# Attention on one Trainium2 core: where TensorE transposes k, before or behind q's projection

## The chip, the core and the metric

The kernel is written in Bass for one core of a Trainium2 chip. The engines named here are PE (TensorE, matmuls and transposes), ACT (ScalarE), DVE (VectorE), POOL (GpSimd) and SP (SyncE, which issues most DMAs). Each runs its own instructions in the order written; semaphores tie them together. The metric is the device time of one execution in microseconds. The kernel before takes 3183.95 us (median of three runs, 3183.66 to 3187.36).

## The reference

A vector of conditions is turned into a gate for x, and the gated x goes through two layers of local attention and a gated feed-forward network; the input is added at the end. All in float32. Cut to the layer:

```python
x: (2, 2048, 512)          # B, N, DIM; 8 heads of 64, windows of 256
x2 = cond(x)               # q.k of the condition, clipped to 0..1, gates v; then Wo
for l in range(2):
    h = shift_token(x2)
    q, k, v = split(h @ wqkv[l])               # 512 columns each
    q, k = l2norm(q) * q_scale, l2norm(k) * k_scale
    q, k = rotary_xpos(q, k)
    o = local_attention(q, k, v)               # softmax over two windows of 256, masked
    x2 = x2 + o @ wo[l]
    h = layernorm(shift_token(x2)) * ln_g + ln_b
    a, g = split(h @ w1[l] + b1[l])
    x2 = x2 + (a * gelu(g)) @ w2[l] + b2[l]
return x + x2
```

## The kernel before, in words

The 4096 rows (2 batches of 2048) are cut into 32 tiles of 128. Stages follow each other: the condition, then for each layer the attention over all 32 tiles, then the feed-forward network in 8 blocks of 4 tiles. Float32 products are made of three passes on rounded parts (`three_passes`, L343 to L347): each operand is split into hi, which ACT copies out of PSUM, and lo, which DVE makes as the difference. So a transpose on PE has two followers: ACT's `a_KT_hi`, `a_QT_hi`, `a_hT_hi` (L1035, L1030, L1026), then DVE's `a_KT_lo`, `a_QT_lo`, `a_hT_lo` (L1332, L1327, L1322).

The attention is a software pipeline written out by hand: `body()` on each engine runs through `STEPS` (t from -1 to 32), and one iteration does pieces of several tiles. On PE an iteration is, in this order: the rest of tile t-1's product with V (`pv`), half of tile t's scores, `p_T(t, 0)`, `v_project(t + 1)`, `p_T(t, 1)`, then the part that is changed, then `pv(t, 0)`, `scores(t + 1, 0)`, `p_T(t, 2)`, `k_project(t + 2)`, `p_T(t, 3)` and `project_out(t - 1)`. The changed part is `k_T(t + 1)` (four transposes of the normed k, L580), `q_project(t + 2)` (12 matmuls, L345 to L347), `q_T(t + 1)` and `h_T(t + 3)` (four transposes each, L580). Below, "the iteration of tile x" is the one with t + 1 = x, in which k and q of tile x are transposed and half of its scores are made.

What the parts wait for: `k_T` for `a_k_normed` (DVE L1317, whose factors POOL's `norms` makes); `pv`'s second half for `a_KT_lo`; `scores` for `a_KT_hi`, `a_KT_lo`, `a_QT_hi` and `a_QT_lo` of its tile. ACT's `body()` has its own fixed order in the same place: `k_T`, `square(0, t + 2)` (the square of the projected q, L1013), `q_T`, `h_T`, `q_copy` (L1017). DVE's is `k_T`, `q_T`, `h_T`. Neither is touched by the change.

At a layer's start, in the iteration of tile 0, there is no softmax work yet: PE does `v_project(0)`, `k_T(0)`, `q_project(1)`, `q_T(0)`, `h_T(2)` and `scores(0, 0)`; the last also waits for POOL's `clear_carry` (four memsets, L1673 and L1674). `q_project(1)` writes bank 2, which the stage before used as well.

Of the kernel before, what the change touches and what calls it, by code (L numbers as in the profile page):

```python
# [25 lines left out]
QUAD = 4  # L26
# [3 lines left out]
START = 1  # L30
# [29 lines left out]
def adaln_ffn_program(nc, x, cond, wqT, bq, wk, bk, wvT, bv, woT, bo,  # L60
# [12 lines left out]
    TILES = B * TB  # L73
    BLOCKS = TILES // QUAD
# [28 lines left out]
    def sem(name):  # L103
        sems.append(ctx.enter_context(nc.semaphore(name)))
        return sems[-1]
# [7 lines left out]
    with ctx:  # L113
# [157 lines left out]
        f_out_set = sem("f_out_set"); f_stored = [sem(f"f_stored{i}") for i in range(QUAD)]  # L271
# [30 lines left out]
        def here(x):  # L302

            return 0 <= x < TILES
# [271 lines left out]
        def _(pe):  # L576
            def transpose_tile(dst, src):

                for k in range(KT_):
                    mm = pe.transpose(dst[:, k * P:(k + 1) * P], src[:, k * P:(k + 1) * P], ident[:])  # L580
                return mm
# [92 lines left out]
            def attention(l):  # L674
                G = l * TILES

                def h_T(x):
                    pe.wait_ge(a_h_in[x % QUAD], START + (l * BLOCKS + x // QUAD + 1) * 32)
                    if x == 1:
                        pe.wait_ge(a_hT_lo, START + G + 1)  # L680
                    if x == 2:
                        pe.wait_ge(a_hT_lo, START + G + 2)
                    if x >= 3:
                        pe.wait_ge(a_PT_lo, START + (G + x - 3) * PAIRS + 2)
                    transpose_tile(h_turn, a_h[:, x % QUAD, :]).then_inc(a_hT_mm, 1)

                def q_T(x):
                    pe.wait_ge(a_q_rotated, START + G + x + 1)
                    if x == 0:
                        pe.wait_ge(a_hT_lo, START + G + 2)  # L690
                    else:
                        pe.wait_ge(a_PT_lo, START + (G + x - 1) * PAIRS + 2)
                    transpose_tile(q_turn, a_qrot[:]).then_inc(a_QT_mm, 1)

                def k_T(x):
                    pe.wait_ge(a_k_normed, START + G + x + 1)
                    if x >= 2:
                        pe.wait_ge(a_O_sum[1], START + GROUPS * (G + x - 1))
                    transpose_tile(k_turn, a_krot[:]).then_inc(a_KT_mm, 1)

                def project(which, x, dst, done):
                    if x == 0:
                        pe.wait_ge(a_w_lo, START + 4 * l + W_ORDER.index(which) + 1)
                    for k in range(KT_):
                        mm = three_passes(pe, dst[:], [a_hT[i][:, x % 2, k, :] for i in range(2)],
                                          [a_w[which][i][:, k, :] for i in range(2)], k == 0, k == KT_ - 1)
                    mm.then_inc(done, 1)
# [10 lines left out]
                def q_project(x):  # L718
                    if x == 0:
                        pe.wait_ge(a_k_copied, START + G + 1)  # L720
                        pe.wait_ge(a_k_squared, START + G + 1)
                    else:
                        pe.wait_ge(a_hT_hi, START + G + x + 1)
                        pe.wait_ge(a_hT_lo, START + G + x + 1)
                    if x >= 2:
                        pe.wait_ge(a_S_masked, START + (G + x - 2) * H + H // 2 + 1)
                    project(0, x, q_work(x), a_q_mm)
# [25 lines left out]
                def scores(x, g):  # L753
                    j = x % QUAD
                    if g == 0:
                        if x == 0:
                            pe.wait_ge(a_carry_zero, START + 4 * l + 4)
                            if l == 0:
                                pe.wait_ge(c_o_set, START + TILES)
                            else:  # L760
                                pe.wait_ge(f_out_set, START + l * BLOCKS * QUAD)
                        elif j == 0:
                            pe.wait_ge(a_carried, START + (l * (BLOCKS - 1) + x // QUAD) * 64)
                        for ready in (a_QT_hi, a_QT_lo, a_KT_hi, a_KT_lo):
                            pe.wait_ge(ready, START + G + x + 1)
                    pe.wait_ge(a_S_masked, START + (G + x) * H + g * H // 2)
                    for i in (2 * g, 2 * g + 1):
                        if i == 3 and x >= 2:
                            pe.wait_ge(a_out_set, START + G + x - 1)
                        if i == 1 and here(x + 1):  # L770
                            pe.wait_ge(a_q_copied, START + G + x + 2)
                            pe.wait_ge(a_q_squared, START + G + x + 2)
                        for step, (q_part, k_part) in enumerate(((0, 0), (0, 1), (1, 0))):
                            for odd in range(2):
                                r = slice(odd * HD, odd * HD + HD)
                                mm = pe.matmul(score_bank(2 * i + odd)[:, 0:WIN * P], a_QT[q_part][r, x % 2, i, :],  # L776
                                               a_KT[k_part][r, i, j * P:(j + WIN) * P], start=(step == 0), stop=(step == 2))
                                if step == 2:
                                    mm.then_inc(a_S_mm, 1)
# [17 lines left out]
                def pv(x, g):  # L797
                    if g == 0:
                        pe.wait_ge(a_V_hi, START + G + x + 1)
                        pe.wait_ge(a_V_lo, START + G + x + 1)  # L800
                        if here(x + 1):
                            pe.wait_ge(a_V_lo, START + G + x + 2)
                    elif here(x + 2):
                        pe.wait_ge(a_k_copied, START + G + x + 3)
                        pe.wait_ge(a_k_squared, START + G + x + 3)
                    pe.wait_ge(a_PT_hi, START + (G + x) * PAIRS + 2 * g + 2)
                    pe.wait_ge(a_PT_lo, START + (G + x) * PAIRS + 2 * g + 2)
                    for odd in range(2):
                        pe.wait_ge(a_O_sum[odd], START + GROUPS * (G + x) + g)
                        if odd == 1 and g == 0 and here(x + 1):  # L810
                            pe.wait_ge(a_KT_lo, START + G + x + 2)
                        for i in range(2):
                            for kb in range(WIN):
                                mm = pe.matmul(o_banks[odd][:, i * 2 * P:(i + 1) * 2 * P],  # L814
                                               a_V[:, x % QUAD + kb, 4 * g + 2 * i + odd, :, :].rearrange("p c d -> p (c d)"),
                                               a_PT[:, 2 * i + odd, kb, :, :].rearrange("p c n -> p (c n)"),
                                               start=(kb == 0), stop=(kb == WIN - 1))
                        mm.then_inc(a_PV_mm[odd], 1)
# [11 lines left out]
                def body():  # L830
                    for t in STEPS:
                        if here(t - 1):
                            pv(t - 1, 1)
                        if here(t):
                            scores(t, 1)
                            p_T(t, 0)
                        if here(t + 1):
                            v_project(t + 1)
                        if here(t):
                            p_T(t, 1)  # L840
                        if here(t + 1):
                            k_T(t + 1)
                        if here(t + 2):
                            q_project(t + 2)
                        if here(t + 1):
                            q_T(t + 1)
                        if here(t + 3):
                            h_T(t + 3)

                        if here(t):  # L850
                            pv(t, 0)
                        if here(t + 1):
                            scores(t + 1, 0)
                        if here(t):
                            p_T(t, 2)
                        if here(t + 2):
                            k_project(t + 2)
                        if here(t):
                            p_T(t, 3)
                        if here(t - 1):  # L860
                            project_out(t - 1)
# [892 lines left out]
```

## Time and profile before

| what | value |
|---|---|
| median of three runs | 3183.95 us |
| the profiled execution, its own time | 3186.28 us |
| its span, first to last instruction | 3184.1 us |
| PE busy | 3071.0 us, 96% of the span |
| DVE, ACT, POOL busy | 58%, 47%, 32% |
| mean granted clock of PE | 0.982 of full speed |

The span is what the profile covers; 2.2 us of the execution lie around it. Busy time says how long an engine had an instruction under way. Matmuls overlap on PE (one starts before the last has ended), so steps between the starts of matmuls say what one costs, not its length. A timeline row gives start, length from first start to last end, engine, line, operation, tiles and count of merged instructions, and in brackets how long the engine had been idle and who ended that.

### The profile page before, as it was taken

To read this page: it belongs to the slowest core of one execution; us is meant where nothing else is said; L and a number is where in the kernel's file an instruction comes from. 1 tells how busy PE (TensorE), PEld (TensorE's weight loads), DVE (VectorE), ACT (ScalarE), POOL (GpSimd) and SP (SyncE) were. 2 spreads that over 40 slices of the span, in tenths; PEclk is the share of its full clock that TensorE was granted. 3 is DMA by queue.
4 is the path that set the end of the run, shared out by engine and by line. 5 is a ranking of instruction groups with operands and counts; after the bars stand their busy time and mean duration, and the time that the engine had idled before them with its cause. 6 is when DMAs were issued, how large, how long until landed. Compare 5 with 4: busy or idle time off the path is not lost.

```text
span 3184.1 us, 48197 instructions
## 1 busy us (share of the span) xinstructions
PE 3071.0 (96%) x16534; PEld 2561.8 (80%) x16534; DVE 1838.7 (58%) x3933; ACT 1484.5 (47%) x3198; POOL 1032.2 (32%) x1671
## 2 busy tenths in 40 slices
PE   9998999999968999999999999999986999999999
PEld 8986888888857788888877888888875788887887
DVE  4655888888864333333324888888875344333432
ACT  2116888888852111111113888888882111111111
POOL 1306666666635000000044566666647000000000
PEclk8999999999989999999999999999997999999999
DMA  4421111222123111100131122111114110111110
GB/s 152 140 78 36 65 60 67 67 67 67 54 77 93 40 40 40 40 8 33 40 121 41 57 68 67 59 65 67 61 59 131 53 36 25 53 47 53 54 40 20
DMA packets 149778, 194.49 MB, mean 61 GB/s; under 512 B 23286, under 2 KB 90998, under 8 KB 149284
## 3 DMA queue, kind: packets, MB, share of 16 engines
q1 hardware_dynamic: 133700, 175.69, 16.8%
q10 hardware_dynamic: 15840, 15.73, 1.5%
q8 instruction: 137, 2.24, 0.3%
q14 instruction: 101, 0.83, 0.1%
HBM read 120.06 MB, written 41.95 MB: 51 GB/s over the span
## 4 chain that ended last, share of the span: by engine, by line
PE 95%; DVE 2%; issue 1%; POOL 1%; ACT 1%; DVEq 0%; SPq 0%; ACTq 0%; POOLq 0%
PE bank L345 25%; PE bank L347 25%; PE bank L346 24%; PE bank L814 6%; PE bank L793 6%; PE bank L776 5%; PE bank L580 3%; PE bank L869 1%; DVE a_PT L1363 0%; PE bank L588 0%; DVE f_h L1481 0%; PE bank L605 0%; ACT a_PT L1074 0%; DVE f_hraw L1489 0%; ACT f_hT_hi L1155 0%
## 5 line engine op out<-in xcount | busy, mean ns | idle before, releaser
L1174 ACT ACTIVATE f_gate<-bank,f_b 128x512 f32<-128x512 f32 (+1 forms) x176 | 121.4, 690 | 997.2 <-PE bank L347 997.1
L345 PE MATMUL bank<-f_hT_hi,f_w_hi 128*128 128x512 f32 (+1 forms) x1408 | 556.5, 395 | 16.3 <-ACT f_hT_hi L1155 15.0
L1517 DVE SCALAR_TENSOR_TENSOR f_uraw<-bank,f_b,f_gate 128x512 f32<-128x512 f32 (+1 forms) x176 | 132.1, 751 | 750.7 <-ACT f_gate L1174 750.5
L347 PE MATMUL bank<-f_hT_hi,f_w_lo 128*128 128x512 f32 (+1 forms) x1408 | 552.9, 393 | 0.0
L346 PE MATMUL bank<-f_hT_lo,f_w_hi 128*128 128x512 f32 (+1 forms) x1408 | 552.0, 392 | 0.0
L345 PEld LDWEIGHTS bank<-f_hT_hi,f_w_hi 128*128 128x128 f32 (+1 forms) x1408 | 260.9, 185 | 78.4 <-ACT f_hT_hi L1155 15.7
L347 PEld LDWEIGHTS bank<-f_hT_hi,f_w_lo 128*128 128x128 f32 (+1 forms) x1408 | 260.6, 185 | 64.2
L346 PEld LDWEIGHTS bank<-f_hT_lo,f_w_hi 128*128 128x128 f32 (+1 forms) x1408 | 261.0, 185 | 62.5
L1069 ACT ACTIVATE a_P<-a_S,a_bias 128x384 f32<-128x384 f32 x512 | 309.4, 611 | 3.9 <-DVE a_bias L1352 3.8
L1352 DVE CUSTOM_DVE_ANT_0 a_S<-bank,a_masks,a_q 128x384 f32<-128x384 f32 x512 | 295.7, 615 | 24.0 <-PE bank L776 18.9
L1062 ACT ACTIVATE a_P<-a_P,a_inv 128x384 f32<-128x384 f32 x512 | 287.3, 613 | 2.1 <-DVE a_inv L1358 0.5
L345 PE MATMUL bank<-f_w_hi,f_u_hi 128*128 128x512 f32 (+1 forms) x704 | 277.6, 394 | 5.1 <-issue 4.3
L1363 DVE TENSOR_TENSOR a_PT<-bank,a_PT 128x768 fp32r<-128x768 f32 x256 | 245.2, 958 | 61.6 <-ACT a_PT L1074 59.0
L347 PE MATMUL bank<-f_w_hi,f_u_lo 128*128 128x512 f32 (+1 forms) x704 | 276.2, 392 | 0.0
L346 PE MATMUL bank<-f_w_lo,f_u_hi 128*128 128x512 f32 (+1 forms) x704 | 275.5, 391 | 0.0
L1074 ACT ACTIVATE a_PT<-bank 128x768 fp32r<-128x768 f32 x256 | 207.8, 812 | 83.0 <-PE bank L793 82.8
L793 PE MATMUL bank<-ident,a_P 128*128 128x128 f32 x1536 | 218.5, 279 | 16.3 <-DVE a_PT L1363 12.1
L793 PEld LDWEIGHTS bank<-ident,a_P 128*128 128x128 f32 x1536 | 174.6, 141 | 66.0 <-ACT a_P L1062 35.4
L1651 POOL CAST a_wk_hi<-a_stage 128x512 fp32r<-128x512 f32 x8 | 5.0, 672 | 686.5 <-DMA a_stage<-in_L_ffn_wqkv 686.5
L814 PE MATMUL bank<-a_PT,a_V 128*128 128x256 f32 x1536 | 212.2, 288 | 9.5 <-DVE a_PT L1363 9.3
L814 PEld LDWEIGHTS bank<-a_PT,a_V 128*128 128x128 f32 x1536 | 198.6, 193 | 16.0 <-issue 10.8
L1521 DVE TENSOR_TENSOR f_u_lo<-f_uraw,f_u_hi 128x512 fp32r<-128x512 f32 (+1 forms) x176 | 127.3, 724 | 122.9 <-ACT f_u_hi L1178 122.9
(166 smaller groups left out, 6559.9 us busy)
## 6 DMA issues: line engine op xcount, KB each, us to landing
a_h<-x_layer_in SPq DMA_DIRECT2D x128, 128.0 KB, 2.8
a_res<-x_layer_in SPq DMA_DIRECT2D x64, 256.0 KB, 2.9
x_after_attention<-out_tiles SPq DMA_DIRECT2D x64, 256.0 KB, 2.0
f_res<-x_after_attention SPq DMA_DIRECT2D x64, 256.0 KB, 3.4
f_stage<-in_L_ffn_w SPq DMA_DIRECT2D x60, 256.0 KB, 3.6
a_V<-a_V SPq DMA_DIRECT2D x28, 512.0 KB, 5.1
f_h<-x_after_attention ACTq DMA_DIRECT2D x28, 512.0 KB, 4.5
c_x<-in_x SPq DMA_DIRECT2D x32, 256.0 KB, 3.1
```

The costliest lines, as they stand in the source:

```text
L345: pe.matmul(dst, w[0], m[0], start=start, stop=False)
L346: pe.matmul(dst, w[0], m[1], start=False, stop=False)
L347: return pe.matmul(dst, w[1], m[0], start=False, stop=stop)
L776: mm = pe.matmul(score_bank(2 * i + odd)[:, 0:WIN * P], a_QT[q_part][r, x % 2, i, :], a_KT[k_part][r, i, j * P:(j + WIN) * P], start=(step ...
L793: mm = pe.transpose(pt_banks[:, odd, kb * P:(kb + 1) * P], a_P[:, (2 * i + odd) % 4, kb * P:(kb + 1) * P], ident[:])
L814: mm = pe.matmul(o_banks[odd][:, i * 2 * P:(i + 1) * 2 * P], a_V[:, x % QUAD + kb, 4 * g + 2 * i + odd, :, :].rearrange("p c d -> p (c d)" ...
L1062: act.activation(a_P[:, h % 4, :], a_P[:, h % 4, :], ACT.Copy, scale=a_inv[:, x % 2, h:h + 1])\
L1069: act.activation(a_P[:, h % 4, :], a_S[h % 2][:], ACT.Exp, bias=a_bias[:, h % 2:h % 2 + 1], scale=-1.0, accum_out=a_sum[:, x % 2, h:h + 1] ...
L1074: act.activation(a_PT[:, 2 * (i % 2):2 * (i % 2) + 2, :, 0, :], pt_banks[:, :, 0:WIN * P].rearrange("p h (k n) -> p h k n", k=WIN), ACT.Co ...
L1352: dve.tensor_tensor_reduce(a_S[b][:], score_bank(h)[:, 0:WIN * P], a_masks[:, min(x % TB, 2), :], a_q8[:, x % 2, h:h + 1], 3.0e38, ALU.add ...
L1363: dve.tensor_tensor(a_PT[:, r, :, 1, :], pt_banks[:, :, 0:WIN * P].rearrange("p h (k n) -> p h k n", k=WIN), a_PT[:, r, :, 0, :], ALU.subt ...
L1517: dve.scalar_tensor_tensor(f_uraw[0:ROWS[m], m % 2, :], bank[pair_of(u, m, end)][0:ROWS[m], :], f_b1[0:ROWS[m], 0, m:m + 1], f_gate[0:ROWS ...
```

## The change

`k_T(t + 1)` moves from before `q_project(t + 2)` to behind it. PE then has the transposes of k, q and h in one row. `q_project(1)` gets a wait of its own for the stage before to have left bank 2: for the last `c_o_set` in layer 0, for the last `f_out_set` of the layer before in layer 1. Until now `k_T(0)`, which stood before it, waited for something that DVE does later than that.

```diff
--- before.py
+++ after.py
@@ -722,6 +722,10 @@
                     else:
                         pe.wait_ge(a_hT_hi, START + G + x + 1)
                         pe.wait_ge(a_hT_lo, START + G + x + 1)
+                    if x == 1 and l == 0:
+                        pe.wait_ge(c_o_set, START + TILES)
+                    elif x == 1:
+                        pe.wait_ge(f_out_set, START + l * BLOCKS * QUAD)
                     if x >= 2:
                         pe.wait_ge(a_S_masked, START + (G + x - 2) * H + H // 2 + 1)
                     project(0, x, q_work(x), a_q_mm)
@@ -838,11 +842,10 @@
                             v_project(t + 1)
                         if here(t):
                             p_T(t, 1)
-                        if here(t + 1):
-                            k_T(t + 1)
                         if here(t + 2):
                             q_project(t + 2)
                         if here(t + 1):
+                            k_T(t + 1)
                             q_T(t + 1)
                         if here(t + 3):
                             h_T(t + 3)
```

PE in the middle of an iteration, before (`a_P` is the softmax, `a_krot` the normed and rotated k, `a_qrot` the rotated q, `a_h` the rows of tile t + 3; where lines are left out, the pattern of three repeats):

```order
L793 MATMUL bank<-ident,a_P 128x128 [waits a_PT_lo,a_P_set]
L793 MATMUL bank<-ident,a_P 128x128 x5
L580 MATMUL bank<-ident,a_krot 128x128 [waits a_O_sum1,a_k_normed]
L580 MATMUL bank<-ident,a_krot 128x128 x3
L345 MATMUL bank<-a_wq_hi,a_hT_hi 128x512 [waits a_S_masked,a_hT_lo,a_hT_hi]
L346 MATMUL bank<-a_wq_lo,a_hT_hi 128x512
...
L347 MATMUL bank<-a_wq_hi,a_hT_lo 128x512
L580 MATMUL bank<-ident,a_qrot 128x128 [waits a_PT_lo,a_q_rotated]
L580 MATMUL bank<-ident,a_qrot 128x128 x3
L580 MATMUL bank<-ident,a_h 128x128 [waits a_PT_lo,a_h_in0]
L580 MATMUL bank<-ident,a_h 128x128 x3
```

And after:

```order
L797 MATMUL bank<-ident,a_P 128x128 [waits a_PT_lo,a_P_set]
L797 MATMUL bank<-ident,a_P 128x128 x5
L345 MATMUL bank<-a_wq_hi,a_hT_hi 128x512 [waits a_S_masked,a_hT_lo,a_hT_hi]
L346 MATMUL bank<-a_wq_lo,a_hT_hi 128x512
...
L347 MATMUL bank<-a_wq_hi,a_hT_lo 128x512
L580 MATMUL bank<-ident,a_krot 128x128 [waits a_O_sum1,a_k_normed]
L580 MATMUL bank<-ident,a_krot 128x128 x3
L580 MATMUL bank<-ident,a_qrot 128x128 [waits a_PT_lo,a_q_rotated]
L580 MATMUL bank<-ident,a_qrot 128x128 x3
L580 MATMUL bank<-ident,a_h 128x128 [waits a_PT_lo,a_h_in0]
L580 MATMUL bank<-ident,a_h 128x128 x3
```

The four transposes of `a_krot` have passed the 12 matmuls with `a_wq`. Their number, their waits and everything around are the same.

ACT beside it, the same before and after (`a_KT_hi` is the copy of k's transposes, `a_sq` the square of the projected q):

```order
L1069 ACTIVATE a_P,a_sum<-a_S,a_bias 128x384 [waits a_PT_mm,a_S_masked] x2
L1035 ACTIVATE a_KT_hi<-bank 128x4x128 [waits a_KT_mm]
L1013 ACTIVATE a_sq<-bank 128x512 [waits a_ss_set,a_q_mm]
L1030 ACTIVATE a_QT_hi<-bank 128x512 [waits a_QT_mm]
L1026 ACTIVATE a_hT_hi<-bank 128x512 [waits a_hT_mm]
L1017 ACTIVATE a_qraw<-bank 128x512 [waits a_q_rotated]
```

ACT takes `a_KT_hi` first, then the square, then `a_QT_hi`; nothing moved here.

PE at the start of layer 0, before (the first row is the end of `v_project(0)`, the last the first scores):

```order
L347 MATMUL bank<-a_wv_hi,a_hT_lo 128x512
L580 MATMUL bank<-ident,a_krot 128x128 [waits a_k_normed]
L580 MATMUL bank<-ident,a_krot 128x128 x3
L345 MATMUL bank<-a_wq_hi,a_hT_hi 128x512 [waits a_hT_lo,a_hT_hi]
...
L347 MATMUL bank<-a_wq_hi,a_hT_lo 128x512
L580 MATMUL bank<-ident,a_qrot 128x128 [waits a_hT_lo,a_q_rotated]
L580 MATMUL bank<-ident,a_qrot 128x128 x3
...
L776 MATMUL bank<-a_KT_hi,a_QT_hi 128x384 [waits a_KT_hi,a_QT_lo,a_KT_lo,a_QT_hi,a_S_masked,c_o_set,a_carry_zero]
```

And after:

```order
L347 MATMUL bank<-a_wv_hi,a_hT_lo 128x512
L345 MATMUL bank<-a_wq_hi,a_hT_hi 128x512 [waits c_o_set,a_hT_lo,a_hT_hi]
...
L347 MATMUL bank<-a_wq_hi,a_hT_lo 128x512
L580 MATMUL bank<-ident,a_krot 128x128 [waits a_k_normed]
L580 MATMUL bank<-ident,a_krot 128x128 x3
L580 MATMUL bank<-ident,a_qrot 128x128 [waits a_hT_lo,a_q_rotated]
L580 MATMUL bank<-ident,a_qrot 128x128 x3
...
L780 MATMUL bank<-a_KT_hi,a_QT_hi 128x384 [waits a_KT_hi,a_QT_lo,a_KT_lo,a_QT_hi,a_S_masked,c_o_set,a_carry_zero]
```

`q_project(1)` now stands before the wait for `a_k_normed` and has a wait for `c_o_set` of its own.

## Rows read from the trace of the kernel before

**Rows 1.** The page: busy time by engine, and the chain that ended last by engine.

```profile
PE 3071.0 (96%) x16534; PEld 2561.8 (80%) x16534; DVE 1838.7 (58%) x3933; ACT 1484.5 (47%) x3198; POOL 1032.2 (32%) x1671
...
PE 95%; DVE 2%; issue 1%; POOL 1%; ACT 1%; DVEq 0%; SPq 0%; ACTq 0%; POOLq 0%
```

**Rows 2.** Stretches: us, busy PE, PEld, DVE, ACT, POOL, clock, DMA share, GB/s.

```profile
250.20:256.40 6.20, 0.19 (x2) 0.04 (x1) 0.79 (x2) 0.60 (x1) 4.79 (x16) 0.68 0.18 68
256.40:259.20 2.80, 2.80 (x9) 2.41 (x10) 1.20 (x2) 0.60 (x1) 2.75 (x5) 0.50 0.00 0
297.00:874.00 577.00, 577.00 (x3695) 494.80 (x3694) 485.56 (x1119) 502.63 (x1175) 361.18 (x644) 1.00 0.19 63
1764.00:2341.00 577.00, 577.00 (x3696) 494.83 (x3695) 485.41 (x1119) 502.74 (x1176) 360.00 (x642) 1.00 0.19 63
```

**Rows 3.** Timeline of PE in the iteration that makes the scores of tile 12, layer 0 .

```profile
503.44 0.81 PE L793 MATMUL bank<-ident,a_P 128*128 128x128 f32 x6
504.09 0.60 PE L580 MATMUL bank<-ident,a_krot 128*128 128x128 f32 x4
504.45 0.48 PE L345 MATMUL bank<-a_wq_hi,a_hT_hi 128*128 128x512 f32 x1
...
507.29 0.60 PE L580 MATMUL bank<-ident,a_qrot 128*128 128x128 f32 x4
507.72 0.60 PE L580 MATMUL bank<-ident,a_h 128*128 128x128 f32 x4
...
509.68 0.44 PE L776 MATMUL bank<-a_KT_hi,a_QT_hi 64*128 64x384 f32 x2
...
514.41 0.82 PE L793 MATMUL bank<-ident,a_P 128*128 128x128 f32 x6
514.99 0.48 PE L345 MATMUL bank<-a_wo_hi,a_OT_hi 128*128 128x512 f32 x1
```

**Rows 4.** Timeline of ACT in the same iteration.

```profile
506.51 0.59 ACT L1035 ACTIVATE a_KT_hi<-bank 128x512 fp32r<-128x512 f32 x1
507.49 0.60 ACT L1013 ACTIVATE a_sq<-bank 128x512 f32<-128x512 f32 x1 [0.39 <-PE bank L347]
507.98 0.59 ACT L1030 ACTIVATE a_QT_hi<-bank 128x512 fp32r<-128x512 f32 x1
...
511.84 0.81 ACT L1074 ACTIVATE a_PT<-bank 128x768 fp32r<-128x768 f32 x1 [0.64 <-PE bank L793]
```

**Rows 5.** Timeline of DVE in the same iteration.

```profile
507.13 0.69 DVE L1332 TENSOR_TENSOR a_KT_lo<-bank,a_KT_hi 128x512 fp32r<-128x512 f32 x1 [0.32 <-ACT a_KT_hi L1035]
508.60 0.69 DVE L1327 TENSOR_TENSOR a_QT_lo<-bank,a_QT_hi 128x512 fp32r<-128x512 f32 x1 [0.78 <-ACT a_QT_hi L1030]
```

**Rows 6.** Timeline near the end of layer 0's loop: QT_lo and the scores of tile 30.

```profile
879.87 0.69 DVE L1327 TENSOR_TENSOR a_QT_lo<-bank,a_QT_hi 128x512 fp32r<-128x512 f32 x1 [0.80 <-ACT a_QT_hi L1030]
...
880.66 0.44 PE L776 MATMUL bank<-a_KT_hi,a_QT_hi 64*128 64x384 f32 x2
```

**Rows 7.** Timeline of layer 0's start: tile 0 (PE, ACT, POOL, PE), then tile 1 (PE).

```profile
256.36 1.11 PE L580 MATMUL bank<-ident,a_krot 128*128 128x128 f32 x4 [6.01 <-DVE a_krot L1317]
...
257.51 0.60 ACT L1035 ACTIVATE a_KT_hi<-bank 128x512 fp32r<-128x512 f32 x1 [6.47 <-PE bank L580]
...
259.14 0.95 POOL L1674 MEMSET a_V<- 128x1024 f32 x1
...
263.29 0.45 PE L776 MATMUL bank<-a_KT_hi,a_QT_hi 64*128 64x384 f32 x2 [1.29 <-issue]
...
277.26 0.66 PE L580 MATMUL bank<-ident,a_krot 128*128 128x128 f32 x4 [2.04 <-DVE a_krot L1317]
```

**Rows 8.** Timeline of layer 1's start: f_res on DVE, PE's first scores, then tile 1's k_T.

```profile
1720.05 2.48 DVE L1536 TENSOR_TENSOR f_res<-bank,f_res 128x512 f32<-128x512 f32 x4 [3.14 <-PE bank L347]
...
1728.76 0.45 PE L776 MATMUL bank<-a_KT_hi,a_QT_hi 64*128 64x384 f32 x2 [1.29 <-issue]
...
1742.75 0.66 PE L580 MATMUL bank<-ident,a_krot 128*128 128x128 f32 x4 [0.46 <-DVE a_krot L1317]
```


## The prediction

> **What bounds the kernel now.** I read the page's busy times and chain first. PE is busy for 96% of the span and carries 95% of the chain that ended last [rows 1], so the question is what the change does to PE's own row of work and which waits it opens or closes there. The busy time by stretch says where PE has slack at all. In the attention loop of either layer, without its ends, PE is busy 577.00 of 577.00 us at a granted clock of 1.00 [rows 2]. That is 28 iterations of 20.6 us without one gap: nothing there waits for k to be normed, and there is nothing to win by covering a wait. Every new delay, on the other hand, is paid in full, once per iteration. Slack stands only at a layer's start, where k_T waits: 6.01 us for tile 0 and 2.04 us for tile 1 in layer 0 [rows 7], 0.46 us for tile 1 in layer 1 [rows 8]. So there are two accounts: the starts, where the change can win, and 28 full iterations per layer, where it can only shift.
>
> **PE's row in a full iteration.** From the starts of PE's instructions [rows 3]: p_T starts at 503.44, k_T at 504.09, q's projection at 504.45, q_T at 507.29, h_T at 507.72, and the scores at 509.68. Behind p_T a projection follows after 0.58 (514.41 to 514.99), where k_T followed after 0.65 and handed over after another 0.36. The projection's 12 matmuls take 507.29 - 504.45 = 2.84. Four transposes that are followed by transposes take 507.72 - 507.29 = 0.43. Before: 0.65 + 0.36 + 2.84 = 3.85 from p_T to q_T. After: 0.58 + 2.84 + 0.43 = 3.85. The change takes no turn between transposes and projection away: there was one into q's projection and one out of it, and there still is. PE's row itself costs 0.00 more or less.
>
> **What the move delays.** k_T now starts at 503.44 + 0.58 + 2.84 = 506.86, which is 2.77 us later. Followed through the other engines:
> - ACT. Before, a_KT_hi ran at 506.51, long after its transposes, in a time when ACT had only PE to wait for; then ACT idled 0.39, and a_sq and a_QT_hi followed at 507.49 and 507.98 [rows 4]. Now a_KT_hi can start only when k_T has ended: 506.86 + 0.60 of length, + 0.04 to ACT (256.36 + 1.11 = 257.47 to 257.51 in rows 7) = 507.50. The square and a_QT_hi stand behind it in ACT's order, at steps of 0.49 (507.49 to 507.98): 507.99 and 508.48. a_QT_hi comes 0.50 later than before although q_T itself is where it was.
> - DVE. a_QT_lo starts 0.62 after a_QT_hi (507.98 to 508.60) and takes 0.69 [rows 4, 5]: now 509.10 to 509.79. a_KT_lo, 0.62 behind a_KT_hi too, ends at 508.81.
> - PE. The scores wait for a_QT_lo. What that handover costs is seen in tile 30, where h_T is missing, and PE comes early: a_QT_lo ends at 879.87 + 0.69 = 880.56 and the scores start at 880.66, so 0.10 [rows 6]. New start of the scores: 509.89 instead of 509.68. **That is 0.21 us of PE per iteration.** pv's second half, which waits for a_KT_lo (508.81), is met too, but its delay ends before the one of the scores and is not added.
>
> Before, a_QT_lo ended at 509.29, and the scores could have started at 509.39: the slack was 0.29, the delay 0.50. That is the whole effect.
>
> What is queued behind: on ACT a_hT_hi, q_copy, tile t's o_copy and normalize go 0.50 later, but ACT had 0.64 idle before the next a_PT copy (511.84 in rows 4), which itself goes 0.21 later; DVE's queue behind a_QT_lo (a_hT_lo, the sums of O, the masks) is taken up in the same gap. k_project has its inputs from the iteration before. So I add nothing for a second stall. The carry DMAs on SP's queue wait for a_KT_lo of every fourth tile; it comes 1.0 us later, with most of an iteration until the carried keys are used: nothing.
>
> Bounds of the 0.21: below, 0 if ACT's queue does not hold the square and a_QT_hi back; above, 0.43, if the two steps on ACT are as long as the instructions (0.60 instead of 0.49). I take 0.21, since each link has a row in this very place.
>
> The Trainium skill states, in "TensorE: Matmul & The Clock Gate", section on the 16 sub-arrays, that ScalarE and VectorE take their queues strictly first in, first out. By that rule a_QT_hi can't pass the waiting a_KT_hi, and the sum stands at 0.21; without it, it would be 0. No row here shows ACT holding back an instruction that was ready, so this is open until the trace after.
>
> **The sum.** Full iterations, tiles 2 to 29 of both layers: 56 x 0.21 = +11.8. Tile 30 of both: there the scores already wait for a_QT_lo, with no slack [rows 6], so the whole 0.50 counts: 2 x 0.50 = +1.0. Tile 31 has no q_project beside it: nothing. Tile 1: PE's wait of 2.04 (layer 0) and 0.46 (layer 1) is now covered by q's projection, 2.84 long; the stall at the scores comes there as elsewhere: -2.5 + 2 x 0.21 = -2.1.
>
> Tile 0 of layer 0: q_project(1) (12 matmuls, which ran mostly at the 0.50 clock [rows 2]) leaves the path behind k_T. k_T stays at 256.36, q_T follows at once; the scores then wait for POOL's last memset, 259.14 + 0.95 = 260.09, so start at about 260.3 instead of 263.29: -3.0 [rows 7]. Against it stands the clock: PE still idles from about 253 (250.2 + 2.84) to 256.4, and has only 12 transposes before 260.3. Before, the granted clock was 0.68 in the idle stretch and 0.50 in the busy one behind it [rows 2], that is, it fell to 1.2 GHz in the idle time and was there for the 2.8 us behind it. Now the scores and k's projection of tile 1 may meet the low clock; of 4.1 us of work at full clock some 1.2 us can be added. I take -3.0 + 1.2 = -1.8, between 0 and -3.0. Tile 0 of layer 1: the f_res additions end at 1722.53 [rows 8], when v_project is just done, so the new wait costs about nothing; q_T comes 0.5 earlier, but a_QT_hi stands behind a_KT_hi, which is now late, and the scores stay at 1728.76: 0.
>
> Total: 11.8 + 1.0 - 2.1 - 1.8 = **+8.9 us**. Against its own time the profiled execution goes from 3186.3 to 3195.2 (span 3184.1 to 3193.0). It was 2.3 us above the median of the runs; I lay the sum on the median: 3183.95 + 8.9 = **3192.8 us**, 0.28% more. Below, "same" means within 0.2%, 6.4 us, about what a measurement of this kernel tells from no change.
>
> **The rivals.**
> - *ACT's order hides it.* If a_QT_hi is not held back by a_KT_hi, or the chain has 0.2 us less than I count, the loops stay at 20.6 us, and only the starts count: -2.5 - 1.8 = -4.3, 3179.7 us. For it: the margin is small against the sum of five links. Against: each link is read from a row. 15%, nearly all within 0.2%.
> - *The stall is twice as large.* DVE's queue behind a_QT_lo (a_hT_lo, sums, masks) goes 0.5 later and the softmax chain gives PE a second wait, or the steps on ACT are longer: 0.43 x 56 = +24, with ends +22, 3206 us. For it: ACT and DVE are busy 503 and 486 of 577 us [rows 2]. Against: 0.64 idle on ACT at the next point. 8%.
> - *Faster, by the row on PE.* If the turn from p_T to q's projection costs less than that from k_T (0.58 against 0.65 + 0.36 with the same four transposes elsewhere), or LDWEIGHTS run ahead better in a row of 12 transposes, each iteration saves up to 0.07 (0.65 against 0.58) and nothing stalls: 60 x 0.07 = -4.2, with the starts -8.5, 3175.5 us. It decides from the point where the scores' wait is under 0.07. Against it: the steps add up to 3.85 either way. 8%.
> - *The clock falls in the row of transposes.* The granted clock is 1.00 through the loop [rows 2], with rows of 10 and 8 transposes in it. At half clock the first k_T took 1.11 instead of 0.60 [rows 3, 7]; 12 transposes so would add some 1.3 us to an iteration, +75 us, 3259. 1%.
>
> **How the numbers follow.** Forecast 68%: its own range, with 0.15 to 0.30 a stall and 0 to -3.0 at tile 0, is +4 to +16; some 50 of the 68 lie above 6.4. Slower: 50 + 8 + 1 = 59%. Same: 18 + 14 = 32%. Faster: 1 + 8 = 9%. For 8 in 10 the range reaches down to the edge of the first rival and up to the end of the forecast's own: 3183 to 3200.
>
> **What would show it.** In the trace after: p_T to q_T still 3.85; a_KT_hi at +4.06 from p_T and a_QT_hi at +5.04 (now +4.54); a PE wait at the scores for DVE's a_QT_lo in nearly each full iteration, and a period of 20.8 instead of 20.6; k_T's waits gone for tile 1. The prediction is wrong in its centre if the period stays at 20.6, or if a wait of PE turns up at p_T or the projections.

## The result, and the profile after

The changed kernel takes 3194.86 us (median of 9 runs, 3193.23 to 3197.12); the kernel before, timed beside it, 3185.52 us (9 runs, 3183.66 to 3190.67). The ratio is 1.0028, with a 95% interval of 1.0019 to 1.0037: slower, by 9.3 us. The prediction said 3192.8 us, 3183 to 3200, and 59% for slower. The profiled execution took 3194.71 us, its span 3192.5 us, 8.4 more than before.

The page of the kernel after, against [rows 1]: busy time by engine, and the chain that ended last.

```profile
PE 3079.8 (96%) x16534; PEld 2564.5 (80%) x16534; DVE 1835.6 (57%) x3933; ACT 1484.0 (46%) x3198; POOL 1032.1 (32%) x1671
...
PE 94%; DVE 2%; issue 1%; POOL 1%; ACT 1%; DVEq 0%; SPq 0%; POOLq 0%; ACTq 0%
```

PE carries 8.8 us more, though it executes the same 16534 matmuls. The stretches of the kernel after (the columns are those of [rows 2]) say where:

```profile
250.20:256.40 6.20, 3.22 (x15) 2.33 (x13) 0.42 (x1) 0.60 (x1) 4.71 (x17) 1.00 0.23 77
256.40:259.20 2.80, 2.47 (x12) 2.42 (x12) 1.56 (x3) 1.32 (x3) 2.75 (x4) 0.50 0.00 0
287.00:294.00 7.00, 6.47 (x37) 5.74 (x38) 4.44 (x12) 5.05 (x13) 5.43 (x18) 0.76 0.01 4
297.00:874.00 577.00, 576.36 (x3655) 491.91 (x3654) 477.75 (x1105) 497.07 (x1164) 356.92 (x628) 1.00 0.19 62
1764.00:2341.00 577.00, 576.19 (x3653) 491.59 (x3652) 478.15 (x1108) 496.87 (x1162) 355.85 (x631) 1.00 0.18 62
```

The loops, which were at 3695 and 3696 instructions in 577 us, now get 3655 and 3653 done: 40 of 3695 fewer is 1.1%, or 0.22 us in 20.62. The busy column hardly says so (576.36 of 577.00): it counts up to the end of a matmul, which the profile models, and matmuls overlap, so a short stall can lie within it. This is the first thing to learn from this case: **on PE read steps and counts, not busy time.** At the start of layer 0, by contrast, PE now does 15 instructions in the first stretch, where there were 2.

PE's timeline of the kernel after, for the iteration of tile 12, as in [rows 3], and p_T and the scores of tile 13:

```profile
503.60 0.82 PE L797 MATMUL bank<-ident,a_P 128*128 128x128 f32 x6
504.17 0.48 PE L345 MATMUL bank<-a_wq_hi,a_hT_hi 128*128 128x512 f32 x1
...
507.00 0.60 PE L580 MATMUL bank<-ident,a_krot 128*128 128x128 f32 x4
507.43 0.60 PE L580 MATMUL bank<-ident,a_qrot 128*128 128x128 f32 x4
507.87 0.60 PE L580 MATMUL bank<-ident,a_h 128*128 128x128 f32 x4
...
510.14 0.45 PE L780 MATMUL bank<-a_KT_hi,a_QT_hi 64*128 64x384 f32 x2
...
524.55 0.82 PE L797 MATMUL bank<-ident,a_P 128*128 128x128 f32 x6
...
530.99 0.44 PE L780 MATMUL bank<-a_KT_hi,a_QT_hi 64*128 64x384 f32 x2
```

Counted from p_T (503.60): q's projection +0.57, k_T +3.40, q_T +3.83 (before: 3.85), scores +6.54 (before: 6.24). In tile 13 the scores come at 530.99 - 524.55 = +6.44. The period is 524.55 - 503.60 = 20.95 behind tile 12 and 20.79 to 20.84 behind those whose scores have no wait for the carried keys; before it was 20.62. ACT and DVE in the same iteration, as in [rows 4] and [rows 5]:

```profile
507.63 0.60 ACT L1038 ACTIVATE a_KT_hi<-bank 128x512 fp32r<-128x512 f32 x1 [0.87 <-PE bank L580]
508.13 0.59 ACT L1016 ACTIVATE a_sq<-bank 128x512 f32<-128x512 f32 x1
508.60 0.61 ACT L1033 ACTIVATE a_QT_hi<-bank 128x512 fp32r<-128x512 f32 x1
...
512.32 0.81 ACT L1077 ACTIVATE a_PT<-bank 128x768 fp32r<-128x768 f32 x1 [0.49 <-PE bank L797]
```

```profile
508.26 0.69 DVE L1335 TENSOR_TENSOR a_KT_lo<-bank,a_KT_hi 128x512 fp32r<-128x512 f32 x1 [1.30 <-ACT a_KT_hi L1038]
509.24 0.69 DVE L1330 TENSOR_TENSOR a_QT_lo<-bank,a_QT_hi 128x512 fp32r<-128x512 f32 x1 [0.29 <-ACT a_QT_hi L1033]
```

a_KT_hi is at +4.03 and a_QT_hi at +5.00; a_QT_lo ends at 509.93, which is +6.33. ACT was idle for 0.87 before a_KT_hi. The square behind it was ready in that time: the last of q's matmuls had ended at 507.16 (506.76 + 0.40), and the sum that it waits for besides (`a_ss_set`) had been made in the iteration before. ACT did not take it before a_KT_hi. That is what the Trainium skill's "TensorE: Matmul & The Clock Gate", in its section on the 16 sub-arrays, says of ScalarE and VectorE (strictly first in, first out); the trace agrees, with a ready instruction held back for 508.13 - 507.16 = 0.97 us.

PE's wait for a_QT_lo is seen best on its weight loads, which stand ahead of the matmuls. Rows of PEld in the kernel after, the scores of tile 12 and of tile 13:

```profile
510.11 0.21 PEld L780 LDWEIGHTS bank<-a_KT_hi,a_QT_hi 64*128 64x128 f32 x2 [0.27 <-issue]
...
530.96 0.22 PEld L780 LDWEIGHTS bank<-a_KT_hi,a_QT_hi 64*128 64x128 f32 x2 [0.16 <-issue]
```

Both have more idle time before them than in the kernel before, where it is 0.13 in the trace, for tile 12 and tile 13 alike (the timeline prints it from 0.15 on). Tile 12's is now 0.11 longer than tile 13's. It is one of the tiles (every fourth) whose scores also wait for the keys that SP carries over (`a_carried`, L767 after). The trace's records of the waiting instructions, which the timeline leaves out, show what that wait does. In tile 13 the instruction that waits for a_QT_lo ends at 530.94, and the weight load starts at 530.96. In tile 12 it ends at 509.98, a further waiting instruction stands from 510.03 to 510.08, and the weight load starts at 510.11. The keys themselves are not late: the last of them had landed 13.4 us before the scores of tile 12, and where PE does not have to wait for a_QT_lo, these tiles take no longer than others (the first experiment, and the kernel before). The fourth tiles show +6.54 to 6.57, but for tile 8 of layer 1 at +6.71, and all others +6.43 to 6.44.

The same by groups, in the loop of layer 0. After (busy us, mean ns, then the idle time before them and who ended it):

```profile
L1335 DVE TENSOR_TENSOR a_KT_lo<-bank,a_KT_hi 128x512 fp32r<-128x512 f32 x28 | 19.4, 692 | 36.5 <-ACT a_KT_hi L1038 36.5
...
L1330 DVE TENSOR_TENSOR a_QT_lo<-bank,a_QT_hi 128x512 fp32r<-128x512 f32 x28 | 19.4, 692 | 8.0 <-ACT a_QT_hi L1033 8.0
```

And in the kernel before:

```profile
L1332 DVE TENSOR_TENSOR a_KT_lo<-bank,a_KT_hi 128x512 fp32r<-128x512 f32 x28 | 19.4, 692 | 8.9 <-ACT a_KT_hi L1035 8.9
...
L1327 DVE TENSOR_TENSOR a_QT_lo<-bank,a_QT_hi 128x512 fp32r<-128x512 f32 x28 | 19.4, 692 | 22.1 <-ACT a_QT_hi L1030 22.1
```

The longer of DVE's two waits was the one at a_QT_lo and is now the one at a_KT_lo: k's copy is now the first of the three to wait for PE, and the two behind it come at ACT's own pace.

The start of layer 0 after (answers to [rows 7]), timeline of PE, ACT, POOL, PE:

```profile
256.73 1.12 PE L580 MATMUL bank<-ident,a_krot 128*128 128x128 f32 x4 [3.31 <-DVE a_krot L1320]
...
257.88 0.60 ACT L1038 ACTIVATE a_KT_hi<-bank 128x512 fp32r<-128x512 f32 x1 [6.49 <-PE bank L580]
...
259.51 0.95 POOL L1677 MEMSET a_V<- 128x1024 f32 x1
...
260.52 0.45 PE L780 MATMUL bank<-a_KT_hi,a_QT_hi 64*128 64x384 f32 x2 [0.96 <-POOL a_V L1677]
```

And tile 1 of layer 0 after, timeline of DVE and PE:

```profile
273.75 0.69 DVE L1320 TENSOR_TENSOR a_krot<-a_krot,a_rs 128x512 f32<-128x512 f32 x1 [2.48 <-POOL a_rs L1614]
...
275.05 0.60 PE L580 MATMUL bank<-ident,a_krot 128*128 128x128 f32 x4
...
276.04 0.95 DVE L1366 TENSOR_TENSOR a_PT<-bank,a_PT 128x768 fp32r<-128x768 f32 x1
...
277.13 0.63 PE L580 MATMUL bank<-ident,a_qrot 128*128 128x128 f32 x4 [1.48 <-DVE a_PT L1366]
...
279.56 0.44 PE L780 MATMUL bank<-a_KT_hi,a_QT_hi 64*128 64x384 f32 x2
```

The waits of k_T for tile 1 are gone (275.05 has none), but q_T now has one that it did not have, 1.48 us.

All shifts in one account, by the starts of PE's instructions in the two profiled executions (after minus before):

| stretch | shift that arises in it, us | predicted |
|---|---|---|
| up to layer 0's attention | +0.35 | 0 |
| layer 0, tiles 0 and 1 (up to p_T of tile 2's iteration) | -2.39 | -3.6 |
| layer 0, tiles 2 to 29 | +6.32 | +5.9 |
| layer 0, tile 30 | +0.48 | +0.5 |
| layer 0, end of the attention and feed-forward | -1.80 | 0 |
| layer 1, tiles 0 and 1 | -2.04 | -0.3 |
| layer 1, tiles 2 to 29 | +6.55 | +5.9 |
| layer 1, tile 30 | +0.45 | +0.5 |
| layer 1, the rest | +0.51 | 0 |
| sum | +8.43 | +8.9 |

### The profile page after: what moved, and what is told of

Read it like the earlier page. It is cut to its first block, busy times and chain, and to the rows that moved or that the text cites. A ratio compares the mean times of both kernels' runs of the same rounds, so it can differ in the third digit from the quotient of the medians.

```text
span 3192.5 us, 48197 instructions
## 1 busy us (share of the span) xinstructions
PE 3079.8 (96%) x16534; PEld 2564.5 (80%) x16534; DVE 1835.6 (57%) x3933; ACT 1484.0 (46%) x3198; POOL 1032.1 (32%) x1671
## 4 chain that ended last, share of the span: by engine, by line
PE 94%; DVE 2%; issue 1%; POOL 1%; ACT 1%; DVEq 0%; SPq 0%; POOLq 0%; ACTq 0%
PE bank L345 25%; PE bank L347 24%; PE bank L346 24%; PE bank L818 6%; PE bank L797 6%; PE bank L780 5%; PE bank L580 3%; PE bank L872 1%; DVE a_PT L1366 0%; PE bank L588 0%; DVE f_h L1484 0%; PE bank L605 0%; ACT a_PT L1077 0%; DVE f_hraw L1492 0%; DVE a_S L1355 0%
## 5 line engine op out<-in xcount | busy, mean ns | idle before, releaser
L818 PE MATMUL bank<-a_PT,a_V 128*128 128x256 f32 x1536 | 222.0, 291 | 10.3 <-DVE a_PT L1366 9.4
```

What stands on the lines that cost most here:

```text
L818: mm = pe.matmul(o_banks[odd][:, i * 2 * P:(i + 1) * 2 * P], a_V[:, x % QUAD + kb, 4 * g + 2 * i + odd, :, :].rearrange("p c d -> p (c d)" ...
```

## The experiments

The theories, as they stand in the expectations: A, ACT's order holds a_QT_hi and so the scores back; B, PE's own row of work costs it; C, only the path over a_QT_lo counts, and pv's wait for a_KT_lo costs nothing; D, starts and ends move with where the granted clock falls; E, DVE's k_norm in front of the softmax's a_PT makes q_T wait in tile 1; F, the added waits, or the place in memory to which they move PE's instructions, change the loop's period.

**The square behind h_T on ACT.** The kernel after, with ACT's square of the projected q moved:

```diff
                         if here(t + 1):
                             k_T(t + 1)
-                        if here(t + 2):
-                            square(0, t + 2)
                         if here(t + 1):
                             q_T(t + 1)
                         if here(t + 3):
                             h_T(t + 3)
                         if here(t + 2):
+                            square(0, t + 2)
                             q_copy(t + 2)
```

> The changed kernel with ACT's square of q moved behind h_T, so that a_QT_hi follows a_KT_hi directly. Theory A (ACT's queue: a_QT_hi is held behind the late a_KT_hi and the square): a_QT_hi starts 4.53 after p_T instead of 5.00, a_QT_lo ends at 5.97 instead of 6.34, and is no longer what the scores wait for; what remains is pv's second half, which waits for a_KT_lo (ends 5.36, pv's half at 5.51, scores 0.88 later at 6.39). The period goes from 20.85 to about 20.78, the time to about 3190.5 us, 0.13% under the changed kernel. Theory B (the row of 12 transposes on PE costs it, and the waits are only its picture): scores stay at 6.43 to 6.54, period 20.85, no change. Theory C (only the path over a_QT_lo counts, the wait of pv costs nothing): scores back at 6.24, period 20.63, 12 to 13 us under the changed kernel.

Measured: 3192.84 us (11 runs), ratio to before 1.0020, 1.0011 to 1.0029; some 3190.5 was expected. The timeline of PE, ACT and DVE, iteration of tile 12:

```profile
504.95 0.81 PE L797 MATMUL bank<-ident,a_P 128*128 128x128 f32 x6
...
508.99 0.60 ACT L1038 ACTIVATE a_KT_hi<-bank 128x512 fp32r<-128x512 f32 x1 [0.88 <-PE bank L580]
...
509.49 0.59 ACT L1033 ACTIVATE a_QT_hi<-bank 128x512 fp32r<-128x512 f32 x1
...
510.23 0.68 DVE L1329 TENSOR_TENSOR a_QT_lo<-bank,a_QT_hi 128x512 fp32r<-128x512 f32 x1
...
511.34 0.44 PE L780 MATMUL bank<-a_KT_hi,a_QT_hi 64*128 64x384 f32 x2
```

a_QT_hi is back at +4.54, as before the change, and a_QT_lo ends at +5.96, before PE gets there. The scores are at +6.39, the period is 20.77 in every tile, the fourth ones included, and the loops are longer than before by 4.1 us each instead of 6.3 and 6.6. So of the stall (0.20 in most iterations, some 0.32 in the fourth ones) undoing ACT's order takes away 0.05, and in the fourth ones also the extra 0.10, since PE no longer waits at the scores: 0.08 in the mean. 0.15 stays. It lies one part earlier: pv's second half, which waits for a_KT_lo, starts at +5.51 instead of +5.43, and its way to the scores is 0.88 instead of 0.81. k's own delay, which the prediction left out of the sum because it ended "before the one of the scores", is thus the larger part of the cost when it stands alone, and hidden behind q's when both are there. The 0.07 lies in one step, by the starts of pv's matmuls in the trace: behind the wait the second one comes 0.19 to 0.20 after the first (510.46 to 510.66, with the weight load at 510.43), where the same step was 0.12 in the kernel before (508.88 to 509.00); all later steps are alike. The changed kernel has the same long step. That the 0.15 is k's lateness and not PE's row is seen in tile 30: h_T is missing there, PE comes 0.43 earlier, and pv's second half still starts at +5.51 and the scores at +6.39. Theory A gave the numbers of the iteration; B and C, as put there, fall. The total came out 2.3 us above what was expected: the loops gave back 4.6 us in the profiles, the spans differ by 2.3, and the rest lies in the starts and ends, which move between executions (see the kernel before again).

**The copy of q ahead of q_T, with PE's order as before.** The kernel before, with one piece of ACT's work moved, so that a_QT_hi is late by 0.5 and nothing changes on PE:

```diff
                         if here(t + 2):
                             square(0, t + 2)
+                        if here(t + 2):
+                            q_copy(t + 2)
                         if here(t + 1):
                             q_T(t + 1)
                         if here(t + 3):
                             h_T(t + 3)
-                        if here(t + 2):
-                            q_copy(t + 2)
```

> The kernel before, PE's order untouched, with ACT's q_copy moved ahead of q_T: a_QT_hi comes one step of ACT (0.49 us) later, at 5.03 after p_T, as in the changed kernel, while a_KT_hi stays early. Theory A: a_QT_lo ends at 6.34, the scores start at 6.44 instead of 6.24, period 20.83, loops +12 us, time some 3197 us with another 0.5 at layer 1's start. Theory B (PE's row of transposes): nothing moves, 3185.5 us. Theory C2 (what costs is a_KT_lo's wait at pv): nothing moves either, 3185.5 us.

Measured: 3204.66 us (4 runs), ratio 1.0055, 1.0041 to 1.0068. The timeline of PE, ACT and DVE, iteration of tile 12:

```profile
509.07 0.82 PE L793 MATMUL bank<-ident,a_P 128*128 128x128 f32 x6
...
513.61 0.59 ACT L1017 ACTIVATE a_qraw<-bank 128x512 f32<-128x512 f32 x1
...
514.08 0.61 ACT L1030 ACTIVATE a_QT_hi<-bank 128x512 fp32r<-128x512 f32 x1
...
514.72 0.69 DVE L1327 TENSOR_TENSOR a_QT_lo<-bank,a_QT_hi 128x512 fp32r<-128x512 f32 x1 [1.29 <-ACT a_QT_hi L1030]
...
515.62 0.44 PE L776 MATMUL bank<-a_KT_hi,a_QT_hi 64*128 64x384 f32 x2 [0.24 <-issue]
```

a_QT_hi is at +5.01, a_QT_lo ends at +6.34, and the scores come at +6.55 in this fourth tile and +6.45 to 6.47 in the others; the loops are longer by 6.8 and 7.0 us. That is the changed kernel's stall, made without touching PE, down to the extra 0.10. Theory B falls here too. In this kernel k's copies are early, and pv's second half starts at +5.43 to 5.46, without the delay of the changed kernel. The total was missed: 17.4 us instead of some 12. The loops give 13.8 of it, and the rest lies in the starts and ends, where ACT's queue is on the path (tile 1's scores in layer 0 come 10.27 after p_T, before 8.52), so this kernel tells about the loop alone.

**The start alone.** k_T stands behind q's projection in tile 0's iteration of each layer, and where it was in all others:

```diff
-                        if here(t + 1):
+                        if here(t + 1) and t > -1:
                             k_T(t + 1)
                         if here(t + 2):
                             q_project(t + 2)
                         if here(t + 1):
+                            if t <= -1:
+                                k_T(t + 1)
                             q_T(t + 1)
```

> k_T behind q's projection at t = -1 alone (tile 0 of each layer), elsewhere as before, with the added waits. Theory A: the loops are back at 20.63 us, tile 0 of layer 0 keeps its gain of 3.1 us (scores at about 260.2 us), tile 0 of layer 1 gains nothing: 3 us under the kernel before, 3182.4 us, ratio 0.999. Rival (the gain at the start is given back in tile 1 by the softmax chain or by the clock): within 1 us of the kernel before.

Measured: 3183.17 us (11 runs), ratio 0.9988, 0.9979 to 0.9997. The loops are back at 20.65 us a period (of that 0.03, below), and the first scores of layer 0 come 12.82 us after v_project(0) began instead of 15.96. The gain at the start is real, though small (the interval ends just under 1), and the loss belongs to the iterations behind it.

**The kernel before again, profiled.** Its one purpose is to see how much two executions of the same kernel differ.

> The kernel before once more, for a second profile. Theory D: the 2.2 us that the changed kernel won at the end of layer 0's attention and the 1.6 us in tile 0 of layer 1 come from where the low clock fell, not from the change: then this profile shows these pieces different from the first profile of the same kernel by 1 us or more, with other stretches of low clock. Rival: they are the same to 0.2 us, and the change did it.

Its span is 3184.6 us, 0.5 more, but the stages differ by more than the sum. Stretches at the start of layer 1 in the first execution of the kernel before:

```profile
1736.00:1742.00 6.00, 5.59 (x23) 4.59 (x24) 2.35 (x7) 4.77 (x11) 4.67 (x16) 0.72 0.00 0
1757.00:1763.00 6.00, 6.00 (x34) 5.08 (x34) 3.50 (x10) 3.77 (x10) 4.51 (x17) 0.72 0.01 3
```

and in this one, with the loop of layer 1 below them:

```profile
1736.00:1742.00 6.00, 3.89 (x24) 3.12 (x21) 2.97 (x8) 5.77 (x16) 5.17 (x11) 1.00 0.00 0
1757.00:1763.00 6.00, 4.72 (x36) 4.15 (x37) 4.60 (x12) 5.26 (x14) 4.96 (x13) 1.00 0.01 3
1764.00:2341.00 577.00, 577.00 (x3692) 494.01 (x3691) 484.42 (x1119) 501.89 (x1173) 360.35 (x640) 1.00 0.19 63
```

The granted clock fell to 1.2 GHz around 1737 and 1757 in the one and at neither in the other (the mean over 6 us is 0.72 and 1.00). This execution was 2.85 us later at tile 1 of layer 0, and only 0.33 at tile 1 of layer 1. Of the two pieces that the expectation names, the one in tile 0 of layer 1 bears theory D out: from its scores to p_T of tile 1's iteration it is 12.72 us in the first execution, 11.11 in this one and 11.13 in the changed kernel. The other, from the end of layer 0's loop to layer 1's start, is only 0.8 shorter here than in the first execution, less than the 1 us that was asked; but in the kernel with the added waits alone (below), whose code there is the same, it is 1.7 shorter. So theory D holds: a shift of 1 to 3 us at a stage's start or end can come without any edit. And one more thing: in layer 1 its period is 20.65 instead of 20.62, with the same code.

**k_norm behind p_T on DVE in tile 1.** The kernel after, with DVE's norming of k(1) moved behind the second a_PT:

```diff
-                        if here(t + 1):
+                        if here(t + 1) and t != 0:
                             k_norm(t + 1)
...
                         if here(t):
                             p_T(t, 1)
                             inverse(t, 3)
+                        if t == 0:
+                            k_norm(1)
```

> The changed kernel with DVE's k_norm(1) moved behind p_T(0, 1) and its inverse, in tile 1's iteration alone. Theory E: in tile 1 q_T waits 1.5 us for a_PT_lo because DVE's queue stands at k_norm(1), which waits 2.5 us for POOL's norms, so that PE's removed wait for k comes back through DVE. Then here a_PT_lo ends about 2.3 us earlier, PE waits about 0.25 for k_norm instead at k_T, q_T starts at 4.1 after p_T instead of 5.49, and the scores of tile 1 at 6.6 to 6.9 instead of 7.92: -1.0 to -1.4 us in either layer where the clock is full. Rival: the softmax chain before it (exp, normalize) is as late, q_T stays at 5.3 or later.

One profiled run, 3196.47 us. The timeline of PE and DVE, tile 1 of layer 0:

```profile
273.28 0.81 PE L797 MATMUL bank<-ident,a_P 128*128 128x128 f32 x6
...
275.28 0.96 DVE L1366 TENSOR_TENSOR a_PT<-bank,a_PT 128x768 fp32r<-128x768 f32 x1
...
276.55 0.69 DVE L1320 TENSOR_TENSOR a_krot<-a_krot,a_rs 128x512 f32<-128x512 f32 x1
...
277.30 0.66 PE L580 MATMUL bank<-ident,a_krot 128*128 128x128 f32 x4 [0.46 <-DVE a_krot L1320]
...
277.79 0.60 PE L580 MATMUL bank<-ident,a_qrot 128*128 128x128 f32 x4
...
280.39 0.45 PE L780 MATMUL bank<-a_KT_hi,a_QT_hi 64*128 64x384 f32 x2
```

a_PT is made in front of a_krot, q_T's wait is gone, and k_T has a small one of 0.46 in its place. The scores come 7.11 after p_T instead of 7.92: 0.8 us won in each layer, somewhat less than the 1.0 to 1.4 expected. Theory E is right in its mechanism.

**Both starts, and k_norm late.** k_T behind q's projection in the iterations of tiles 0 and 1 (`t > 0` and `t <= 0` in place of `t > -1` and `t <= -1` above), with the edit on DVE:

> k_T behind q's projection at t = -1 and t = 0 alone, with DVE's k_norm(1) late as in the run before; the loops as in the kernel before. Theory E: 3.1 us at tile 0 and 1.6 us at tile 1 of layer 0, about 0.2 in layer 1: 4.9 us under the kernel before, ratio 0.9985. Rival: tile 1 gives nothing back, then as with t = -1 alone, ratio 0.999.

Measured: 3181.57 us (11 runs), ratio 0.9988, 0.9979 to 0.9997; 0.9985 was expected. The loops have a period of 20.62. It is 0.12% faster than the kernel before and 0.4% faster than the changed one (13.3 us between the medians of different sets of runs), but it can't be told from the kernel with tile 0's start alone.

**The added waits alone.** The kernel before, with the wait for `c_o_set` and `f_out_set` in q_project(1) and nothing else:

```diff
+                    if x == 1 and l == 0:
+                        pe.wait_ge(c_o_set, START + TILES)
+                    elif x == 1:
+                        pe.wait_ge(f_out_set, START + l * BLOCKS * QUAD)
```

> The kernel before with the added waits at q_project(1) alone. Theory: they are met before PE comes there, no change, period 20.63. Rival F (what moved the period from 20.625 to 20.655 in the run with k_T behind at t = -1 alone is where PE's instructions lie in memory, moved by the added waits): period 20.65, +0.8 us per layer, not to be seen in the time.

Measured: 3185.32 us (10 runs), ratio 1.0000, 0.9991 to 1.0009. Layer 0's period is 20.62, layer 1's 20.65. Since the kernel before shows both periods too, without these waits, theory F falls: no cost of the waits is to be seen.

**The kernel after again, profiled.**

> The changed kernel once more, for a second profile. Theory D: periods as before to 0.01 us (20.82 to 20.95, the long ones at every fourth tile), while the ends of the attention stages and the starts differ by 1 us or more with where the low clock fell.

One run, 3199.53 us, 4.8 more than the first profiled one. The periods are 20.81 to 20.85 and, behind the fourth tiles, 20.91 to 20.95, as in the first (one of 21.13, behind tile 8 of layer 1, has its like there too, 21.10); both loops together, tiles 2 to 29, take 1168.1 us here, 1167.8 in the first and 1154.9 before. The 4.8 us lie in the starts and ends. A stretch at layer 1's start here, where the first execution of this kernel had the full clock:

```profile
1757.00:1763.00 6.00, 3.58 (x20) 3.17 (x19) 3.96 (x11) 4.85 (x13) 4.06 (x4) 0.81 0.00 0
```

And at the start of layer 0 there were ten microseconds of low clock (255.4 to 265.7) instead of three (256.4 to 259.8): the first scores come 12.8 after v_project(0) in both, but p_T of tile 1's iteration only 0.71 earlier than in the kernel before, where the first execution had 2.76.

## Why the prediction came out as it did

The forecast was the likeliest case, and its mechanism is shown. But the sum of +8.9 against a measured +8.4 in the profiles (+9.3 between the medians) is closer than its terms deserve. By its own steps:

- **p_T to q_T 3.85, PE's row costs nothing**: 3.83 to 3.84. Right. Of the 0.07 that a rival had PE save, there is 0.01 to 0.02, and the stall takes it.
- **a_KT_hi at +4.06, a_QT_hi at +5.04, a_QT_lo's end at +6.35, the scores at +6.45**: 4.03, 5.00, 6.33, 6.43 to 6.44. Right, each link within 0.04.
- **56 x 0.21 = +11.8**: measured 6.32 + 6.55 = +12.9. The mechanism was right, the size short in one point: every fourth tile costs 0.10 more, since another waiting instruction stands behind the one for a_QT_lo. I had read `a_carried` in the code and costed the transfer, not the wait. 14 such tiles give 1.4 us; what is left is 56 x 0.205.
- **pv's second half "is not added"**: right as a sum, wrong as a picture. Undoing ACT's part alone leaves 0.15 of the stall, where "the whole effect" was said to be a_QT_lo's lateness. Two causes overlap, and only the later one was priced.
- **Tile 30, 2 x 0.50**: 0.48 and 0.45. Right.
- **Tile 0 of layer 0, -3.0 and +1.2 for the clock**: the first scores came 3.12 earlier by the stage's own start. The clock gave back nothing in the first execution (-3.11 still at p_T of tile 1's iteration), and 2.5 in the second of the same kernel (-3.14 at the scores, -0.59 at p_T, both counted from v_project(0)). But the reference moves too. From v_project(0) to p_T of tile 1's iteration the order before takes 27.07, 30.12 and 29.64 us (its two profiles and that with the added waits), the order after 23.95, 26.49, 26.44, 26.27, 26.34 and 25.51 (its two profiles and the four experiments that have it there). In the mean that is 3.1 less, with nothing given back to the clock: low stretches cost the old order as well, and the 1.2 charged to the new order alone finds no support in these nine. No single pair of executions can check it.
- **Tile 0 of layer 1, 0**: 0.02. Right.
- **Tile 1, -2.1**: wrong, and the one step whose mechanism failed. Layer 0's scores came 0.60 earlier relative to p_T, not 1.83 (2.04 less the stall of 0.21); layer 1's came at +7.93, against +6.93 where the clock had made PE late before, and +8.50 in the second execution. I followed what waits for k_T, and not what stands in DVE's queue behind the k_norm that k_T had waited for: the masks, a_V, and the a_PT that q_T needs. In the kernel before a_PT was as late (278.80 + 0.94), but q_T, behind k_T and the projection, came at 280.52 and did not see it. With the wait at k_T gone, that was next: 1.48 us. The move of k_norm shows it. The rest of that iteration, from the scores to p_T of tile 2's, was 1.3 us longer than before in layer 0 (15.6 against 14.3) and 1.5 shorter in layer 1; that is the clock, which was low at 287 to 291 after and at 1757 to 1761 before, and not the change.
- **Starts and ends of the stages, 0**: they moved by -0.9 in sum at places that the change doesn't touch (+0.35, -1.80, +0.51), and layer 1's start by -2.0 instead of -0.3, where the kernel before had two low stretches of the clock and after none. That hid the error at tile 1 and the missing 1.1 of the loops. Without these stretches the change costs more: the second executions of both kernels, 12.7 us apart in span, show as much on the other side, and the medians, 9.3 apart, lie between.

The rivals. ACT's order hiding the move (15%) is refuted by the held-back square and by the period. A stall twice as large (8%) did not come: ACT's idle time before the next a_PT went from 0.64 to 0.49, and no second wait showed. The clock fell at no row of 12 transposes: it is at 1.00 in both loops.

What stays open: what makes the period 20.65 instead of 20.62 in some layers of some executions (q_T at +3.87 instead of +3.85, by hundredths in each projection), in the kernel before as well. The code is the same. Nor is it known why the changed kernel has one iteration 0.2 us longer than its like, behind tile 8 of layer 1, in both executions; the trace only shows where: between the two waiting instructions in front of the scores, which lie 0.23 apart there and 0.06 in the other fourth tiles. No experiment took the wait for the carried keys away by itself; that the fourth tiles' 0.10 vanishes with the wait for a_QT_lo and appears with it, on either order of PE, is shown.

## What to carry to other kernels

- An instruction that is moved on one engine takes its followers with it on every engine whose queue has a fixed order. The copy of k stood in front of the copy of q on ACT; moving k's transposes next to q's made q late, though q's transposes had not moved. Move the followers as well, or leave it; and add up what the moved work itself delays: with a_QT_hi back at its old place 0.15 of 0.23 us stayed, for the late k.
- Where PE has no slack in the loop, and slack in the first iterations, treat these apart: the same edit was worth -3 us at layer 0's start and +13 us in the loops. Alone at the start it gave 0.12%.
- When a wait goes, look up what is queued behind its releaser too: the engine that was waited for may hold the next input in the same queue.

## What the runs showed of the hardware that was not expected

- One more waiting instruction behind a wait that ends late costs PE 0.10 to 0.11 us (idle time before the weight load 0.27 instead of 0.16), though the keys had landed 13.4 us before; where PE does not wait there, it costs nothing (+6.24 in the fourth tiles of the kernel before as in the others).
- Behind a wait the step from PE's first matmul of pv's second half to the next is 0.19 to 0.20 us, where it is 0.12 in a running row. So a wait of 0.08 costs 0.15.
- A loop of 28 iterations of the same code can settle at 20.62 or at 20.65 us, in the same kernel.
- Low stretches of the granted clock at the stages' starts and ends fall at other places from one execution to the next. They moved single stages by 1 to 3 us, and the whole by up to 4.8 us: as much as half of what this change costs. Here the loops, at 1.00 throughout, are what can be compared between two traces.
